# A two-layer cross-attention kernel: the first layer's 16x16 attention over heads is softened in two halves, with earlier projections and smaller POOL products

## The reference, cut to what matters

```python
def _L0_ffn_ref(x, ...):                      # D = 256, H = 16, HD = 16, L = 64, E = 8
    h = _rmsnorm(x, gamma1)
    q = (h @ Wq + bq).reshape(b, t, H, HD)
    kv = ((h @ Wdown + bdown) @ Wup + bup).reshape(b, t, H, 2 * HD)
    k, v = jnp.split(kv, 2, axis=-1)
    att = jnp.einsum('bthd,btgd->bthg', q, k) / np.sqrt(HD)
    att = jax.nn.softmax(att, axis=-1)
    out = jnp.einsum('bthg,btgd->bthd', att, v).reshape(b, t, D)
    x = x + (out @ Wo + bo)
    h2 = _rmsnorm(x, gamma2)
    gate = jax.nn.softmax(h2 @ Wg + bg, axis=-1)
    combined = jnp.einsum('btd,edf,bte->btf', h2, We, gate)
    return x + combined

x = x + tanh(g_xattn[0]) * _L0_xattn_ref(_layernorm(x), ctx, ctx, mask, ...)   # 16 heads of 64, causal
x = x + tanh(g_ffn[0]) * _L0_ffn_ref(_layernorm(x), ...)
# the second layer: cross-attention with 16 heads of 16, a two-expert feed-forward part
```

## Time and profile before

| | |
|---|---|
| profiled execution | 2663.2 us |
| its span | 2661.4 us |
| PE busy | 2325.5 us (87%) |
| DVE busy | 1487.3 us (56%) |
| ACT busy | 1268.0 us (48%) |
| POOL busy | 1019.5 us (38%) |
| POOL's products with v, L364, x64 | 287.4 us, mean 4527 ns, idle before them 180.7 us, for DVE L637 |
| POOL's products of q and k, L350, x64 | 290.3 us, mean 4547 ns |
| DVE's reductions of them, L643 and L620, x64 each | 146.3 and 145.9 us |

### The profile page before, as it was taken

How to read it: one execution, slowest core, us unless ns; L and a number is a source line. 1 busy time by engine, 2 the same in 40 slices (tenths; PEclk the granted TensorE clock), 3 DMA queues, 4 the chain that set the end, 5 groups by cost and what they waited for, 6 DMA issues and landing times. The chain is left out here.

```text
span 2661.4 us, 48220 instructions
## 1 busy us (share of the span) xinstructions
PE 2325.5 (87%) x16128; PEld 1931.7 (73%) x16128; DVE 1487.3 (56%) x3906; ACT 1268.0 (48%) x3971; POOL 1019.5 (38%) x910
## 2 busy tenths in 40 slices
PE   5888989888888898888466999999999999999998
PEld 4667777777777777776354777877777887777777
DVE  3467667666766676767635445444444544444441
ACT  5655566555556555556023444433344443334441
POOL 1355554555554455555512333222233322223320
PEclk9989999999999999999667999999999999999999
DMA  4000000000000000000040000000000000000000
GB/s 145 14 6 17 13 16 4 16 16 16 16 12 4 16 16 16 16 4 9 4 161 1 13 17 16 16 16 16 4 12 16 16 16 16 16 4 12 16 9 9
DMA packets 25856, 51.66 MB, mean 19 GB/s; under 512 B 6272, under 2 KB 7040, under 8 KB 24640
## 3 DMA queue, kind: packets, MB, share of 16 engines
q1 hardware_dynamic: 25792, 50.84, 5.7%
HBM read 42.44 MB, written 8.39 MB: 19 GB/s over the span
## 5 line engine op out<-in xcount | busy, mean ns | idle before, releaser
L1191 POOL TENSOR_SCALAR l_probs<-l_probs,l_rinv 128x256 f32<-128x256 f32 x512 | 238.4, 480 | 590.0 <-DVE l_rinv L1406 589.4
L1302 ACT ACTIVATE l_probs<-l_score,l_negmax 128x256 f32<-128x256 f32 x512 | 238.4, 472 | 265.0 <-DVE l_negmax L1401 265.0
L364 POOL TENSOR_TENSOR l_prod<-l_att,l_kv 128x2048 f32<-128x2048 f32 x64 | 287.4, 4527 | 180.7 <-DVE l_att L637 180.7
L350 POOL TENSOR_TENSOR l_prod<-l_q,l_kv 128x2048 f32<-128x2048 f32 x64 | 290.3, 4547 | 155.9 <-DVE l_att L620 84.1
L1606 PE MATMUL l_ffn<-l_w,l_hid 128*128 128x256 f32 x1536 | 347.9, 382 | 1.0 <-ACT l_hid L1276 1.0
L1606 PEld LDWEIGHTS l_ffn<-l_w,l_hid 128*128 128x128 f32 x1536 | 287.6, 190 | 51.0 <-issue 14.3
L1413 DVE COPY l_probsT<-l_attn 128x512 f32<-128x512 f32 x256 | 175.5, 685 | 161.1 <-PE l_attn L1569 160.9
L710 DVE CUSTOM_DVE_ANT_0 l_probs<-l_score,l_mbias 128x256 f32<-128x256 f32 (+1 forms) x512 | 161.3, 353 | 147.5 <-PE l_score L906 97.6
L1401 DVE TENSOR_REDUCE l_negmax<-l_score 128x2 f32<-128x512 f32 x256 | 175.1, 684 | 65.4 <-PE l_score L1557 65.4
L643 DVE TENSOR_REDUCE l_h<-l_prod 128x128 f32<-128x2048 f32 x64 | 146.3, 2286 | 110.7 <-POOL l_prod L364 110.7
L439 ACT ACTIVATE l_probs<-l_probs,l_negmax 128x256 f32<-128x256 f32 x256 | 130.8, 511 | 107.7 <-DVE l_negmax L710 106.5
(11 more groups left out here) (271 smaller groups left out, 7527.2 us busy)
## 6 DMA issues: line engine op xcount, KB each, us to landing
l_ctxin<-in_ctx SPq DMA_DIRECT2D x32, 256.0 KB, 3.0
l_xin<-in_x SPq DMA_DIRECT2D x16, 256.0 KB, 2.7
l_x<-in_x SPq DMA_DIRECT2D x16, 256.0 KB, 2.6
x<-l_acc SPq DMA_DIRECT2D x16, 256.0 KB, 2.0
l_xin<-x SPq DMA_DIRECT2D x16, 256.0 KB, 3.3
l_x<-x SPq DMA_DIRECT2D x16, 256.0 KB, 2.6
out<-l_x SPq DMA_DIRECT2D x16, 256.0 KB, 2.0
l_hid<-in_w SPq DMA_DIRECT2D x2, 1536.0 KB, 8.6
```

What stands on the lines that cost most here:

```text
L350: nc.gpsimd.tensor_tensor(prod[:, u].rearrange("p (h g d) -> p h g d", h=half, g=H), q4[:, u * half:(u + 1) * half].unsqueeze(2).to_broadc ...
L364: nc.gpsimd.tensor_tensor(prod[:, u].rearrange("p (h d g) -> p h d g", h=half, d=HD), a4.unsqueeze(2).to_broadcast([P, half, HD, H]), v4.u ...
L1191: last = nc.gpsimd.tensor_scalar(probs[:, j % 4, t * S:(t + 1) * S], probs[:, j % 4, t * S:(t + 1) * S], rinv[:, j, t:t + 1], 1.0, ALU.mul ...
L1302: last = nc.scalar.activation(probs[:, s % 4, t * S:(t + 1) * S], ps[:, t * S:(t + 1) * S], ACT.Exp, bias=negmax[:, s, t:t + 1], accum_out ...
```

## The change

Four things, all in `layer0`:

1. The pieces of b stand earlier: hT in step 1 (was 2), down and then q in step 2 (were 4 and 3), up0 in step 3 (was 5), up1 in step 4 (was 6). The order of the side banks follows.
2. The reductions of the four score products stand in steps 6, 7, 9 and 10 (were 7, 9, 11, 12).
3. The softmax is taken for each half of the tokens, 128 of them with 16x16 scores: maximum, subtraction on DVE in steps 7 and 10, exponential on ACT beside the same steps (so at the head of steps 8 and 11, behind the copies of projections), divide on DVE in steps 8 and 11. It was one softmax over both halves in steps 12 and 13. The gathers stand in steps 11, 13, 14 and 16 (were 15, 16, 18, 19). `weigh` waits for its half's divide, and its first two products also for the reductions that free their buffers.
4. POOL issues each product of 2048 elements as four instructions of 512 (`PART = 2` heads each); the last one increments the semaphore.

```diff
-        mix_at = {2: "hT", 3: "q", 4: "down", 5: "up0", 6: "up1"}
+        mix_at = {1: ("hT",), 2: ("down", "q"), 3: ("up0",), 4: ("up1",)}
...
-        score_at = {7: 0, 9: 1, 11: 2, 12: 3}
-
-        gather_at = {15: 0, 16: 1, 18: 2, 19: 3}
+        score_at = {6: 0, 7: 1, 9: 2, 10: 3}
+        soften_at, divide_at = {7: 0, 10: 1}, {8: 0, 11: 1}
+        gather_at = {11: 0, 13: 1, 14: 2, 16: 3}
...
 # POOL, query_key
-                    nc.gpsimd.tensor_tensor(
-                        prod[:, u].rearrange("p (h g d) -> p h g d", h=half, g=H),
-                        q4[:, u * half:(u + 1) * half].unsqueeze(2).to_broadcast([P, half, H, HD]),
-                        k4.unsqueeze(1).to_broadcast([P, half, H, HD]), ALU.mult).then_inc(prod_ready, 1)
+                    out = prod[:, u].rearrange("p (h g d) -> p h g d", h=half, g=H)
+                    for h in range(0, half, PART):
+                        last = nc.gpsimd.tensor_tensor(
+                            out[:, h:h + PART], q4[:, u * half + h:u * half + h + PART].unsqueeze(2).to_broadcast([P, PART, H, HD]),
+                            k4.unsqueeze(1).to_broadcast([P, PART, H, HD]), ALU.mult)
+                    last.then_inc(prod_ready, 1)
...
 # POOL, weigh (its product is cut in the same way)
+                    if u == 0:
+                        pool.wait_ge(att_ready, 2 * b + t + 1)
                     if piece < 2:
-                        pool.wait_ge(att_ready, b + 1)
+                        pool.wait_ge(scored, 4 * b + piece + 3)
                     else:
                         pool.wait_ge(gathered, 4 * b + piece - 1)
...
 # ACT, beside_head
-                    if b is not None and s == 12:
-                        act.wait_ge(sub_ready, b + 1)
-                        nc.scalar.activation(att[:], att[:], ACT.Exp, scale=HD ** -0.5).then_inc(aexp_done, 1)
                     if a is not None and s in own_at:
                         project(own_at[s], a)
                     if nxt is not None and s in ahead_at:
                         project(ahead_at[s], nxt)
+                    if b is not None and s in soften_at:
+                        t = soften_at[s]
+                        act.wait_ge(sub_ready, 2 * b + t + 1)
+                        nc.scalar.activation(att[:, t], att[:, t], ACT.Exp, scale=HD ** -0.5).then_inc(aexp_done, 1)
...
 # DVE (mix_softmax_divide in the same way, for half t)
+                def mix_softmax_max(b, t):
+                    att3, of = heads_of(t)
+                    dve.drain()
+                    V.tensor_reduce(amax[:, of], att3, axis=AX.X, op=ALU.max)
+                    dve.drain()
+                    V.tensor_tensor(att3, att3, amax[:, of].unsqueeze(2).to_broadcast([P, H, H]), ALU.subtract).then_inc(sub_ready, 1)
...
 # DVE, beside_head
                         if s in score_at:
                             mix_scores(b, score_at[s] // 2, score_at[s] % 2)
-                            if score_at[s] == 3:
-                                mix_softmax_max(b)
-                        if s == 13:
-                            dve.drain()
-                            mix_softmax_divide(b)
+                        if s in soften_at:
+                            mix_softmax_max(b, soften_at[s])
+                        if s in divide_at:
+                            mix_softmax_divide(b, divide_at[s])
                         if s in gather_at:
                             mix_gather(b, gather_at[s])
...
 # PE, beside_head
-                        elif use == "q":
-                            side.emptied(pe, "hT", b)
-                            tokens(side, "q", b, hT, fq, D)
-                        elif use == "down":
-                            mix_down(b)
+                            elif use == "q":
+                                tokens(side, "q", b, hT, fq, D)
+                            elif use == "down":
+                                side.emptied(pe, "hT", b)
+                                mix_down(b)
```

More of the change, by code:

```diff
@@ L30 @@
 LAT = 64
+PART = 2
 E = 8
@@ L198, in layer0 @@
         attn = Banks(nc, ctx, "l0_attn", attn_uses + ["out"], ahead=["xT", "k0", "k1", "k2", "v0", "v2"])
[L200 removed]
+        mix_at = {1: ("hT",), 2: ("down", "q"), 3: ("up0",), 4: ("up1",)}
         expert_at = {6: 0, 7: 1, 8: 2, 10: 3, 12: 4, 14: 5, 15: 6, 17: 7}
         add_at = {7: 0, 8: 1, 9: 2, 10: 3, 12: 4, 14: 5, 15: 6, 17: 7}
[L203 to L205 removed]
+        score_at = {6: 0, 7: 1, 9: 2, 10: 3}
+        soften_at, divide_at = {7: 0, 10: 1}, {8: 0, 11: 1}
+        gather_at = {11: 0, 13: 1, 14: 2, 16: 3}
         score = Banks(nc, ctx, "l0_score", [f"s{j}" for j in range(H)] + ["idle0", "idle1"], 3)
         heads = Banks(nc, ctx, "l0_heads", [f"o{j}" for j in range(4)], 1)
[L208 removed]
+        mix_uses = ["hT", "down", "q", "up0", "up1", "idle"]
         moe_uses = ["oT", "out", "h2T", "gate"] + [f"we{j}" for j in range(E)]
         side = SideBanks(nc, ctx, "l0_side", mix_uses, moe_uses,
[L211 removed]
+                         ["oT", "out", "hT", "down", "q", "up0", "up1", "h2T", "gate"] + [f"we{j}" for j in range(E)] + ["idle"])
         raw_in, split_hi, split_lo = [sem("raw_in0"), sem("raw_in1")], sem("split_hi"), sem("split_lo")
@@ L363, in weigh @@
                     a4 = att[:, t].rearrange("p (h g) -> p h g", g=H)[:, u * half:(u + 1) * half]
-                    nc.gpsimd.tensor_tensor(prod[:, u].rearrange("p (h d g) -> p h d g", h=half, d=HD),
-                                            a4.unsqueeze(2).to_broadcast([P, half, HD, H]), v4.unsqueeze(1).to_broadcast([P, half, HD, H]),
-                                            ALU.mult).then_inc(prod_ready, 1)
+                    out = prod[:, u].rearrange("p (h d g) -> p h d g", h=half, d=HD)
+                    for h in range(0, half, PART):
+                        last = nc.gpsimd.tensor_tensor(out[:, h:h + PART], a4[:, h:h + PART].unsqueeze(2).to_broadcast([P, PART, HD, H]),
+                                                       v4.unsqueeze(1).to_broadcast([P, PART, HD, H]), ALU.mult)
+                    last.then_inc(prod_ready, 1)
                 def body(a, b, c, nxt):
@@ L470, in before_exp @@
                 def before_exp(b, c, s):
-                    if b is not None and mix_at.get(s) == "hT":
+                    if b is not None and "hT" in mix_at.get(s, ()):
                         high(side, "hT", b, hT[0], hT_hi, gamma1)
-                    if b is not None and mix_at.get(s) == "down":
+                    if b is not None and "down" in mix_at.get(s, ()):
                         ps, full, _, turn = side.at("down", b)
@@ L737, in beside_head @@
                             V.tensor_copy(x1res[:], x1[:]).then_inc(x1_copied, 1)
[L738 to L741, removed]
-                        elif use == "q":
-                            mix_queries(b)
-                        elif use == "down":
-                            mix_down(b)
-                        else:
-                            mix_kv(b, int(use[2:]))
+                    if b is not None:
+                        for use in mix_at.get(s, ()):
+                            if use == "hT":
+                                low(side, "hT", b, hT, hT_hi, gamma1)
+                            elif use == "q":
+                                mix_queries(b)
+                            elif use == "down":
+                                mix_down(b)
+                            else:
+                                mix_kv(b, int(use[2:]))
                     if c is not None:
```

38 lines of the change are left out of this document (18 added, 20 removed).

## The result

The changed kernel takes 2748.8 us (median of 4 runs, 2745.86 to 2755.92), the kernel before 2658.06 beside it (2657.45 to 2660.88): ratio 1.034, 95% interval [1.0322, 1.0364]. It is slower by 90.7 us; +54 was forecast. The profiled execution took 2755.92 us with a span of 2754.1, against 2663.2 and 2661.4. By the starts of PE's transposes of the mixed heads, the 14 bodies that have a, b and c went from 1097.5 us together (166.04 to 1263.55) to 1188.4 (167.57 to 1355.99): +90.9 of the 92.7 between the spans. The first body that has a b, whose front has no c, ends 1.5 later; the body without attention is 0.9 longer; the second layer is the same to 0.6. So the place was right, and the question is a steady body: 78.4 on average before, 84.9 after.

The account below looks back on a forecast made before the run. PE was taken as the bound, working 68.67 of 78.36 us per body, the rest waits. Terms summed to +3.8 per body, +57 over 15 bodies, -3 for the body without attention: +54, so 2712 us, range 2665 to 2755.

Parts of the forecast that it names:

- the forecast case: The prediction's main case for the whole kernel: 2712 us, own range 2665 to 2755, chance 0.66.
- PE, steps 1 to 5, +1.7: First-layer body: earlier projections make PE wait for h and h2T, less waits that go; +1.7 us per body.
- DVE and ACT, steps 7 to 11, +1.0, +1.25, +0.85: Half softmax in step 7, half divide in step 8, then the path to v0: these three additions in us per body.
- blocked operations, +2.6: Four DVE operations on the path (xn, softmax subtractions, multiplication) wait for POOL's pieces, 0.65 us each: +2.6 us per body.
- The tail, -3.6: From v0 to the next body: 22.15 us plus 0.5 for a last wait, against 26.26; -3.6 us per body.
- Sum, +3.8: All per-body terms of the first layer together: +3.8 us per body, +57 us over 15 bodies.
- TensorE's clock: A new wait in step 9 may bring another lower-clock stretch: costed at 0, at 1.5 us without cover by xT's wait.
- The body without attention, -3: First-layer body with b and c only: POOL's eight products follow one another at 5.0 us each, saving 3 us.
- faster: Rival: DVE's added work in steps 7 and 8 fits existing waits, PE does not stand for probsT 5; 2627 us, chance 0.19.
- pieces that do nothing: Rival: DVE is not let in between POOL's pieces and waits for the whole product; 2823 us, chance 0.06.
- At 1.27 for each blocked operation: Upper bound for DVE operations blocked by POOL, one 512-element piece each: 15 x 6.3 - 3 = +91, 2750 us.

Follow-up runs that it names:

- the filled run: The changed kernel with thrown-away matmuls in three of PE's waits (ahead of hT, gate, and heads 4 and 5): 2712.8 us, ratio 1.020.

## Why the prediction was right, and where its size was off

The time fell into the forecast case's own range (2665 to 2755), at its upper end. What it named as decisive is there: PE waits 4.14 in step 9 for ACT's copy, where "2 to 4 us" stood; hT waits 1.87 (1.5 to 2); xn takes 1.76 (over 1); ACT stands twice a body on the subtraction; nothing waits before oT. The body is 85.5, not 80 to 84.

- **PE, steps 1 to 5, +1.7**: right, 1.69 with the projections alone. gate 1.51 for 1.4, down 0.46 for 0.4; in the changed kernel down does not wait, since PE comes to it out of a stretch at the lower level.
- **DVE and ACT, steps 7 to 11, +1.0, +1.25, +0.85, and blocked operations, +2.6**: with the front they put v0 at 52.1 + 1.7 + 3.1 + 2.6 = 59.5 into the body. The run with the clock of before has it at 59.25. Within that, the four blocked ones on the path cost 3.15 and not 2.6: 1.76 - 0.74 for xn, 1.03 - 0.43 and 0.93 - 0.43 for the subtractions, 1.46 - 0.43 for the first multiplication. The other terms must then be some 0.8 too large together; which ones, no run separates.
- **The tail, -3.6**: right. From v0 to the next body there are 22.77 us (570.22 to 592.99), 23.05 in the filled run, for 22.65.
- **Sum, +3.8**: at the clock of before the measured body is 82.30 - 78.36 = +3.94.
- **TensorE's clock, "I cost it at 0, since PE then waits for xT anyway"**: this is the step that failed. The prediction saw one new stretch coming, and gave a price of 1.5 for the case without cover; there are three more, one of them of twice the length. The wait that was to cover them, ahead of k1, took up 1.4 us of what they cost: it is 2.78 in the filled run and 1.35 in the changed kernel. It took up no more, as the low part of xT, for which PE waits, comes 2.8 us later too (k1 starts 53.48 into the changed body and 50.65 into the filled one). Filled with other work, the waits cost 3.2 us per body less: 36 us in the run, nearly the whole distance from 2712 to 2749. The cover that the kernel before does have stands ahead of oT, as two of its bodies behind each other show:

```profile
324.05:402.39 78.34, 70.15 (x490) 58.17 (x489) 54.64 (x154) 45.44 (x142) 42.44 (x17) 0.96 0.04 14
402.39:480.75 78.36, 68.66 (x490) 56.96 (x489) 54.79 (x155) 45.44 (x142) 42.46 (x17) 0.98 0.04 14
```

The first has 1.49 more of PE's busy time and no wait ahead of the oT that ends it, the second has 1.51 there, and they last the same. The change takes this wait away, and with it the cover.

- **The body without attention, -3**: wrong, +0.9. POOL's products did come closer together, but the first subtraction stood through five pieces (last section), and the reduction of the third product, behind it on DVE, came so late that POOL idled for 5.7 us ahead of the weighing. In the filled run the same subtraction takes 1.01, POOL does not idle there, and this body is 4.2 shorter than before. So the term failed by one blocked operation; a hold of 7 us stood nowhere in the prediction.

Of the rivals, "faster" decided at whether PE waits for probsT 5, and it does. What whole products cost shows that "pieces that do nothing" would have been worse than priced: 2859 for 2823. At 1.27 for each blocked operation the prediction had 2750, and that agrees with the time by accident: the operations did not cost that much.

## What to carry to other kernels

Where engines execute in written order, a short instruction that waits costs what stands behind it, so a softmax moved forward on DVE and ACT has to be priced at the copy behind it that PE needs. A new wait on PE has two prices, its own length and the matmuls at half the clock that may stand around it; whether a later wait hides the second has to be asked of that wait as it will be, not as it is: the change may take it away. And a wait that can be filled with thrown-away matmuls tells in one run how much of a loss is the clock, if no stretch comes elsewhere instead.

## What the runs showed of the hardware that was not expected

**Pieces do not always let DVE in.** In the steady body the subtraction that starts at 548.37 begins inside POOL's first piece of four (547.87 to 549.12) and ends at 549.40, 0.28 after that piece. In the body without attention (no a) POOL's timeline from 1384 to 1394 and DVE's rows are these:

```profile
1383.05 9.76 POOL L353 TENSOR_TENSOR l_prod<-l_q,l_kv 128x512 f32<-128x512 f32 x8
```

```profile
1386.04 7.06 DVE L640 TENSOR_TENSOR l_att<-l_att,l_amax 128x256 f32<-128x256 f32 x1
...
1402.13 0.42 DVE L640 TENSOR_TENSOR l_att<-l_att,l_amax 128x256 f32<-128x256 f32 x1
```

POOL's eight pieces run without a gap until 1392.81, and the subtraction, which starts within the third, ends only at 1393.10. With pieces of 256 the same subtraction takes 8.20. Beside no product the operation takes 0.42 (the run with one softmax); the second subtraction here takes as little, as it starts 0.12 before a piece ends (1401.00 to 1402.25) and is let in. At 549 and at 1386 alike a piece followed at once. That two whole products stood in POOL's queue in the second case, and one in the first, is not the reason: in the filled run the same body has the same sixteen pieces without a gap, the subtraction starts in the same piece, the third of the third product, and DVE is let in.

```profile
1338.30 20.03 POOL L353 TENSOR_TENSOR l_prod<-l_q,l_kv 128x512 f32<-128x512 f32 x16 [6.61 <-DVE l_kv L624]
1351.09 1.01 DVE L640 TENSOR_TENSOR l_att<-l_att,l_amax 128x256 f32<-128x256 f32 x1
```

Nor is it this body alone: with the projections back, the last body with an a has a subtraction of 7.05, which ends 0.28 after the last of POOL's sixteen pieces. So a subtraction beside pieces of 512 takes 1.0 or 7 us, and what decides it stays open.

**The clock's stretches move.** Half the clock came in stretches of some 3.5 us, or 6.9 around the 4.14 us wait. Filling the wait ahead of k1 in the kernel before took the stretch away there, and one of the same length came in step 5 of the body shown, where nothing had been changed and no wait is over 1.02. Which wait a stretch belongs to can't be read from its place alone.
